# First attention of a two-layer block: the order of an iteration's steps on TensorE

## What is computed

```python
q = lat @ Wq                                   # lat: layer norm of x, (4, 512, 128)
kv = jnp.concatenate([ctx, lat], axis=1) @ Wkv # ctx: layer norm of the context, (4, 32, 128)
k, v = jnp.split(kv, 2, axis=-1)               # split_heads: 16 heads of 64
dots = jnp.einsum('bhid,bhjd->bhij', q, k) * scale
attn = jax.nn.softmax(dots, axis=-1)
out = jnp.einsum('bhij,bhjd->bhid', attn, v)   # heads joined again
return out @ Wout
...
x = x + first_attention(ctx, layernorm(x))
x = x + experts_b(layernorm(x))                # one expert of 8 for a row
x = x + second_attention(layernorm(x), ctx)
x = x + experts_d(layernorm(x))                # two experts of 8 for a row
```

## Time and profile before

| | |
|---|---|
| median of 3 runs | 792.72 us (792.16 to 794.59) |
| profiled execution, span | 798.2 us |
| PE busy | 713.8 us (89%) |
| DVE busy | 491.6 us (62%) |
| ACT busy | 366.9 us (46%) |
| POOL busy | 378.2 us (47%) |
| mean granted clock of PE | 0.948 |
| chain that ended last | PE 75%, DVE 8%, issue 6% |

### The profile page before, as it was taken

The page is one execution under the profiler, slowest core; times in us unless marked ns, Lnnn a source line. Parts: engine busy times, 40 slices in busy tenths (PEclk is TensorE's granted clock), DMA queues, the critical chain, the costliest instruction groups (busy, mean ns, idle before and its releaser), DMA issues.

```text
span 798.2 us, 13900 instructions
## 1 busy us (share of the span) xinstructions
PE 713.8 (89%) x4626; PEld 414.0 (52%) x4626; DVE 491.6 (62%) x1077; ACT 366.9 (46%) x572; POOL 378.2 (47%) x369
## 2 busy tenths in 40 slices
PE   4899999999999999999999999987995587659991
PEld 4655556545556545555545455454664244326660
DVE  4655484595594875675775666664442477746673
ACT  5465554564654553654554643432332543314440
POOL 6254453553563573464375454524222314765552
PEclk9999999999999999999999999999998688569996
...
DMA packets 69132, 50.45 MB, mean 63 GB/s; under 512 B 4068, under 2 KB 62312, under 8 KB 69064
## 3 DMA queue, kind: packets, MB, share of 16 engines
...
...
## 4 chain that ended last, share of the span: by engine, by line
PE 75%; DVE 8%; issue 6%; POOL 4%; ACT 3%; DMA 2%; another core or an unknown queue 1%; SPq 1%; DVEq 0%; POOLq 0%; ACTq 0%
PE PSUM L1602 14%; PE PSUM L1634 13%; PE PSUM L1444 7%; PE PSUM L1569 5%; PE PSUM L1469 4%; PE PSUM L1700 4%; PE PSUM L1403 4%; PE PSUM L1407 3%; PE PSUM L1409 2%; PE PSUM L1408 2%; PE PSUM L1583 2%; PE PSUM L1576 2%; PE PSUM L1620 2%; PE PSUM L1664 2%; POOL results_d L643 2%
## 5 line engine op out<-in xcount | busy, mean ns | idle before, releaser
L838 ACT ACTIVATE PT<-PSUM 128x1024 f32<-128x1024 f32 x128 | 128.7, 1025 | 134.2 <-PE PSUM L1602 133.9
L671 POOL TENSOR_TENSOR PSUMS<-PT 128x1024 f32<-128x1024 f32 x32 | 76.1, 2378 | 210.6 <-ACT PT L838 171.6
L671 POOL TENSOR_TENSOR PSUMS<-PSUMS,PT 128x1024 f32<-128x1024 f32 x62 | 149.7, 2415 | 16.6 <-ACT PT L838 9.7
L1235 DVE TENSOR_REDUCE TOPS<-PSUM 128x2 f32<-128x1024 f32 x128 | 152.0, 1220 | 7.4 <-PE PSUM L1569 7.0
L1634 PE MATMUL PSUM<-PT,BIG 128*64 128x512 f32 x512 | 130.6, 611 | 0.6 <-issue 0.6
L1444 PE MATMUL PSUM<-BIG,XGT 128*128 x170 | 86.5, 614 | 2.4 <-issue 1.6
L1225 DVE TENSOR_TENSOR KL<-PSUM,KH 128x512 fp32r<-128x512 f32 x32 | 22.1, 692 | 68.0 <-ACT KH L816 67.5
L1189 DVE TENSOR_TENSOR SIL<-SIL,PSUM 128x256 f32<-128x256 f32 (+1 forms) x62 | 32.1, 518 | 48.0 <-ACT SIL L758 45.4
L1569 PE MATMUL PSUM<-KH,QH 64*128 64x512 f32 x256 | 58.0, 449 | 3.9 <-DVE QL L1228 3.6
L1634 PEld LDWEIGHTS PSUM<-PT,BIG 128*64 128x64 f32 x512 | 28.4, 135 | 54.0 <-issue 52.5
L1602 PE MATMUL PSUM<-QH,KH 64*128 64x512 f32 x256 | 54.9, 424 | 1.0 <-DVE QL L1228 0.8
...
## 6 DMA issues: line engine op xcount, KB each, us to landing
...
```

The costliest lines, as they stand in the source:

```text
L671: pool.tensor_tensor(PSUMS[:, i % 2], PTT[:, i % 2, 0] if kt == 1 else PSUMS[:, i % 2], PTT[:, i % 2, kt], ALU.add).then_inc(s_ps, 1)
L838: act.activation(PTT[:, i % 2, kt], PSUM[:, place:place + 2, :], ACT.Exp, scale=DH ** -0.5).then_inc(s_exp, 1)
L1235: dve.tensor_reduce(TOPS[:, c, 0, :], PSUM[:, place:place + 2, :], AX.X, ALU.max).then_inc(s_max, 1)
```

## The change

`ITERATION` is written anew. In the words of its names an iteration on PE is now: V, qk, mt, P0, P2, PC, the small steps of router and norm (128x128 but for PC); then p0 p1 p2 p3; then OUT, rows, CS; then t0 s0 t1 s1 t2 s2 t3 s3 t4. `max_turn` is split: DVE's part becomes `max_joined` (mj) at the end of the iteration, and the turn itself (mt) comes behind the next iteration's qk. `one_over` is split into the copy on ACT (`one_half`), four reciprocals spread over the iterations k+1 and k+2 (k = 4(g+1)), and the low part on DVE (`one_low`), which gets a wait for the former group's `spread`. `context_sums` and `context_add` take one half in iteration k and one in k+1; `spread`, `out` and `add` move from k+1 and k+2 to k+3. Steps of norm and router move by up to an iteration. Because qk of a group's first pair now comes before CS of the group before it, the queries' copy gets a fifth place, QF1.

```diff
--- before.py
+++ after.py
@@ -105,7 +105,7 @@
 
 
         with ExitStack() as queries:
-            QF = queries.enter_context(nc.sbuf_tensor("QF", [P, GROUP, S], F32))
+            QF4 = queries.enter_context(nc.sbuf_tensor("QF4", [P, GROUP, S], F32))
             TOPROW = queries.enter_context(nc.sbuf_tensor("TOPROW", [P, GROUP, S], F32R))
         BIG = sb("BIG", 3, KT * INNER)
         V = BIG[:, 1:3, :].rearrange("p k (t n) -> p k t n", t=KT)
@@ -169,6 +169,7 @@
             QL = sb1("QL", 2, S)
             KH = sb1("KH", 2, S)
             KL = sb1("KL", 2, S)
+            QF1 = first.enter_context(nc.sbuf_tensor("QF1", [P, S], F32))
 
         W2ALL = sb("W2ALL", E * F_B)
         SIL = sb("SIL", 3, BANK)
@@ -317,8 +318,7 @@
 
 
         ITERATION = (
-            "E A B PC CA0 C CA1 O0 ADD CS V qk p0 p1 t0 s0 t1 p2 t2 D s1 t3 p3 t4 P0 P2 s2 s3 rows mt O1 OUT "
-            "O2 O3").split()
+            "O C V qk mt P0 P2 PC B E A CA R p0 p1 D p2 p3 OUT ADD rows CS t0 s0 t1 s1 H t2 s2 t3 s3 t4 mj RL").split()
 
         beside = [{} for _ in range(ALL + 1)]
 
@@ -326,56 +326,60 @@
             beside[i].setdefault(at, []).append((name, a))
         for g in range(2 * B):
 
-            put(GROUP * g + GROUP - 1, "CS", "context_scores", g)
-            for half in range(2 if g < 2 * B - 1 else 0):
-                put(GROUP * (g + 1) + 1, "PC", "context_sums", (g, half))
-                put(GROUP * (g + 1) + 1, f"CA{half}", "context_add", (g, half))
+            k = GROUP * (g + 1)
+            put(k - 1, "CS", "context_scores", g)
+            if g == 2 * B - 1:
+                break
+            for half in range(2):
+                put(k + half, "PC", "context_sums", (g, half))
+                put(k + half, "CA", "context_add", (g, half))
+            put(k, "H", "one_half", g)
+            put(k + 1, "O", "one_over", (g, 0))
+            put(k + 2, "O", "one_over", (g, 1))
+            put(k + 2, "R", "one_over", (g, 2))
+            put(k + 2, "R", "one_over", (g, 3))
+            put(k + 2, "RL", "one_low", g)
+            put(k + 3, "P0", "spread", GROUP * g)
+            put(k + 3, "P2", "spread", GROUP * g + 2)
+            put(k + 3, "OUT", "out", g)
+            put(k + 3, "ADD", "add", g)
         for b in range(B + 1):
             i = b * PAIRS
-            if 2 <= b:
-                put(i, "A", "r0_slot", b - 2)
-                put(i, "D", "r0_send", b - 2)
             if b == B:
                 break
             if b + 1 < B:
-                put(i, "E", "a_stats", b + 1)
-                put(i, "A", "a_rstd", b + 1)
-                put(i + 1, "D", "a_out", b + 1)
+                put(i + 1, "E", "a_stats", b + 1)
+                put(i + 1, "A", "a_rstd", b + 1)
+                put(i + 2, "D", "a_out", b + 1)
                 put(i + 3, "C", "a_turn", b + 1)
                 put(i + 3, "D", "a_split", b + 1)
                 for kt in range(KT):
                     put(i + 4 + kt, "V", "values", (b + 1, kt))
-            for g in (2 * b - 1, 2 * b):
-                if g >= 0:
-
-                    k = GROUP * (g + 1) + 1
-                    for c in range(4):
-                        put(k, f"O{c}", "one_over", (g, c))
-                    put(k + 1, "P0", "spread", GROUP * g)
-                    put(k + 1, "P2", "spread", GROUP * g + 2)
-                    put(k + 1, "OUT", "out", g)
-                    put(k + 2, "ADD", "add", g)
             if b > 0:
                 put(i + 4, "E", "r0_stats", b - 1)
                 put(i + 4, "A", "r0_rstd", b - 1)
-                put(i + 4, "D", "r0_out", b - 1)
-                put(i + 5, "D", "r0_turn", b - 1)
+                put(i + 5, "D", "r0_out", b - 1)
+                put(i + 6, "C", "r0_turn", b - 1)
                 put(i + 6, "B", "r0_logits", b - 1)
-                put(i + 6, "C", "r0_top", b - 1)
-                put(i + 7, "A", "r0_hot", b - 1)
-                put(i + 7, "D", "r0_run", b - 1)
+                put(i + 6, "B", "r0_top", b - 1)
+                put(i + 6, "A", "r0_hot", b - 1)
+                put(i + 7, "C", "r0_run", b - 1)
+                put(i + 7, "A", "r0_slot", b - 1)
+                put(i + 7, "D", "r0_send", b - 1)
 
         first_top = [("top", (0, c)) for c in range(TOPS_OF)]
         order = [("qk", 0), ("context_keys", 1)] + first_top[0:2] + [("values", (0, 0))] + first_top[2:4] + [("values", (0, 1))]
-        order += first_top[4:] + [("max_turn", 0), ("context_kept", 1), ("counters", 0)]
+        order += first_top[4:] + [("max_joined", 0), ("max_turn", 0), ("context_kept", 1), ("counters", 0)]
 
         instead = [[("values", (0, 2))], [], [("values", (0, 3))], [("context_values", 0), ("spread_rounded", 0)]]
         for i in range(ALL):
             for at in ITERATION:
                 if at[0] == "s":
                     order.append(("scores", (i, int(at[1]))))
-                elif at in ("qk", "mt") and i + 1 < ALL:
-                    order.append(("qk" if at == "qk" else "max_turn", i + 1))
+                elif at in ("qk", "mj") and i + 1 < ALL:
+                    order.append(("qk" if at == "qk" else "max_joined", i + 1))
+                elif at == "mt" and i:
+                    order.append(("max_turn", i))
                 elif at[0] == "t" and i + 1 < ALL:
                     order.append(("top", (i + 1, int(at[1]))))
                 elif at[0] == "p":
@@ -392,8 +396,8 @@
 
         b = B - 1
         rest = [("e_tables", 0), ("kv_copies", 0), ("context_sums", (last, 0), 2, 2), ("rows", ALL - 1), ("context_add", (last, 0)),
-                ("one_over", (last, 0))] + [("pv", (ALL - 1, kt)) for kt in range(KT)]
-        rest += [("one_over", (last, c)) for c in range(1, 4)] + [("context_sums", (last, 1), 4, 2), ("context_add", (last, 1)),
+                ("one_half", last), ("one_over", (last, 0))] + [("pv", (ALL - 1, kt)) for kt in range(KT)]
+        rest += [("one_over", (last, c)) for c in range(1, 4)] + [("one_low", last), ("context_sums", (last, 1), 4, 2), ("context_add", (last, 1)),
                  ("e_tables", 2), ("masks", 0)]
         rest += [("kv", 0), ("kv_kept", 0), ("spread", GROUP * last, 0, 2), ("spread", GROUP * last + 2, 4, 2), ("ex", 0), ("ex", 1),
                  ("ek", 0), ("ek", 1), ("e_tables", 3), ("out", last, 0, 1), ("add", last), ("eg", 0), ("r0_stats", b), ("r0_rstd", b),
@@ -421,6 +425,10 @@
 
         scored = [(name, a) for name, a, place, banks in order_a if name in ("scores", "context_scores")]
         SCORED = {step: i + 1 for i, step in enumerate(scored)}
+
+        def query(i):
+
+            return QF4[:, i % (GROUP + 1), :] if i % (GROUP + 1) < GROUP else QF1[:, :]
 
         def scores_of(i):
             return SCORED["scores", (i, KT - 1)]
@@ -814,9 +822,9 @@
                         act.wait_ge(s_sc, scores_of(a - 2))
                     act.activation(QH[:, a % 2, :], PSUM[:, place, :], ACT.Copy).then_inc(s_qkh, 1)
                     act.activation(KH[:, a % 2, :], PSUM[:, place + 1, :], ACT.Copy).then_inc(s_qkh, 1)
-                    if a >= GROUP:
-                        act.wait_ge(s_sc, context_of(a // GROUP - 1))
-                    act.activation(QF[:, a % GROUP, :], PSUM[:, place, :], ACT.Copy).then_inc(s_qkh, 1)
+                    if a > GROUP:
+                        act.wait_ge(s_sc, context_of((a - 1) // GROUP - 1))
+                    act.activation(query(a), PSUM[:, place, :], ACT.Copy).then_inc(s_qkh, 1)
                 elif name == "max_turn":
                     act.wait_ge(s_topt, a + 1)
                     if a >= GROUP:
@@ -849,8 +857,8 @@
                     if i >= OTS:
                         act.wait_ge(s_out, (i - OTS) // GROUP + 1)
                     act.activation(OT[:, i % OTS, :], PSUM[:, 6, :], ACT.Copy).then_inc(s_ot, 1)
-                elif name == "one_over" and a[1] == 0:
-                    g = a[0]
+                elif name == "one_half":
+                    g = a
                     act.wait_ge(s_rows, GROUP // 2 * (g + 1))
                     if g:
                         act.wait_ge(s_recl, g)
@@ -1237,7 +1245,7 @@
                         dve.tensor_reduce(TOPS[:, :, 1, :].rearrange("p t h -> p h t"),
                                           PSUM[:, place:place + 2, 0:TPB * M].rearrange("p h (t n) -> p h t n", t=TPB),
                                           AX.X, ALU.max).then_inc(s_max, 1)
-                elif name == "max_turn":
+                elif name == "max_joined":
                     dve.wait_ge(s_max, TOPS_OF * (a + 1))
                     if a:
                         dve.wait_ge(s_topt, a)
@@ -1253,12 +1261,15 @@
                         dve.tensor_tensor(REC[0:64, :], REC[0:64, :], PSUM[64:128, 7, :], ALU.add).then_inc(s_sums, 1)
                         dve.wait_ge(s_sums, g + 1)
                     dve.reciprocal(REC[0:64, cols], REC[0:64, cols]).then_inc(s_rec, 1)
-                    if c == 3:
```

(17 more changed lines are left out.)

## The result

| | before | after |
|---|---|---|
| median, same chip | 793.65 us (4 runs) | 833.63 us (831.68 to 835.61, 4 runs) |
| profiled execution, span | 798.2 us | 830.0 us |
| mean granted clock of PE | 0.948 | 0.944 |

The changed kernel takes 1.0496 times as long (95% interval 1.0466 to 1.0526): 40 us more, where 18.8 were forecast and the range ended at 821.

A forecast was written before the change was run, and what follows sets the result against it. PE's own stream bounds the kernel (busy 100.00 of 100 us). Terms -19.5 + 31 + 12.4 - 2.1 + 1 + 2.4 - 5.4 - 1 = +18.8 us on the 792.72 median gave 811.5 us; range 797 to 821.

The forecast's parts named there:

- crossings and block, net, 31 plain iterations: PE's loop: fewer shape changes save 19.5 us, waits in the block of maxima and scores cost 31 us.
- P2's wait less the crossings of P0 and P2: Behind mt: P2 waits for QL to free qk's place, 12.4 us in all; shape changes no longer needed save 2.1.
- PC, OUT, CS: Shape changes: CS loses one of its own, OUT and the split PC gain one each; plus 1 us, within 2.
- waits of before that go, last iteration: Today's waits of t1 and t4 go, minus 5.4 us; fewer crossings in the last iteration, minus 1.
- the third block: t0 to t4 at the iteration's end: s1, t3 and s3 wait for their places, 1.0 us an iteration.
- rival without waits (780): DVE and ACT free the places in time for s1, t3 and s3, so 31 us fall away: 780; chance 0.12.
- The maxima's turn: ... mt does not wait: mt behind qk: the maxima are joined 0.7 us behind t4, the projections take 1.5, so no wait.
- takers between qk and P2 are mt and P0 alone: PSUM places behind qk: the argument against P2 not waiting, a rival of 799 us with chance 0.06.
- at clock 1.00: Attention after the change: PE's busy share falls from 100 to about 93, its clock stays at 1.00.
- the reciprocals behind the router's steps (2.4): DVE, iterations 14, 22 and 30: reciprocals come 0 to 1.7 us late behind router steps; 2.4 us in all.
- Rows had 0.4 us of slack: rows ahead of the third block: GpSimd's adds end at 11.5, PE arrives at 11.9; cost 0.
- DVE comes late ... in more iterations, +10: Rival: about 14 iterations start the third block 0.5 to 1 us late, rows waits for GpSimd; 821, chance 0.12.

The follow-up runs named there:

- e5: Changed kernel with DVE's maxima over the scores reading 256 of 512 keys: 817.60 us, ratio 1.0286 to the kernel before.
- e6: Kernel before with DVE's maxima over the scores reading 256 of 512 keys: 795.27 us, ratio 1.0014.
- e8: Changed kernel with GpSimd's second and third add of each iteration over 64 of 512 columns: 813.84 us, ratio 1.0247 to before.
- e3: Changed kernel with P0 and P2 between p1 and p2 instead of behind the maxima's turn: 817.72 us, ratio 1.0306 to before.
- e2: Changed kernel with the router's counts moved from the iteration's head to behind qk and the maxima's turn: 828.29 us, ratio 1.0360 to before.
- e4: Changed kernel with 12 filler matmuls ahead of the maxima's turn in iterations 15 and 23: 834.63 us, ratio 1.0444 to before.
- e7: Changed kernel with p2 and p3 again between the turns of maxima and scores, rows ahead of them: 839.77 us, ratio 1.0506 to before.
- e12: Changed kernel reordered: pv in two visits, P0, P2 and whole context sums ahead of projections, router's counts behind them, rows late: 790.06 us, ratio 0.9953 to before.

## Why the prediction was right and wrong

| term | forecast | measured |
|---|---|---|
| crossings and block, net, 31 plain iterations | +11.5 | +8.7 |
| P2's wait less the crossings of P0 and P2 | +10.3 | +11.5 |
| PC, OUT, CS | +1 | +8.6 |
| router and norm: their steps, and waits ahead of max_turn and P0 | +2.4 | +13.5 |
| pv at the lower clock | 0 | +6.7 |
| waits of before that go, last iteration | -6.4 | -8.6 |
| sum | +18.8 | +40.4 |

(The terms measured come from the table by step; the plain iteration's shares, rounded, make the 0.4 too much. "Waits of before that go" is what is left of top and scores, +8.5, less 31 plain shares of 0.55.)

**Right: the direction, the block and P2.** The starts of the third block came out within 0.07 us, each of six, and its waits as 0.92 where 0.99 was derived. e5 and e6 show the mechanism: the same edit gives 2.1% in after, nothing in before. The rival without waits (780) falls; it needed a block wait below 0.4 us. The Trainium skill, page "TensorEngine Tiling (Array Packing)", section Performance Considerations, warned of the emptying of PSUM, and the trace agrees: 1.22 us of DVE and 1.02 of ACT stand behind each turn. P2's wait was derived rightly too, 1.88 a time: in e8, where P0 comes on time, P0 and P2 take 2.98 instead of 1.12 us six times over.

**Luck in one row: +10.3 forecast, +11.5 measured.** In after P2's six waits are smaller than derived, since P0 is late itself: spread is 8.4 us above before in the six iterations, of which e3 takes back 6.9. The other 3.1 are iteration 31, where the prediction had 0.5 for the router's counts and P2 waited 1.9 for PLACE, at the lower clock. The row agrees because one error made up for another.

**Wrong: "OUT and the split PC gain one each", 0.15 for a PC.** I counted the split as a second visit. It is a second full run, 1.02 us for half the matmuls, +7.7. The trace of before held 16 records in 1.04, and the code says which rows each half uses; I did not put the two together.

**Wrong: "The maxima's turn: ... mt does not wait", and P0 at nothing.** mt does not wait for the maxima, right; but it waits for its place. I had followed the place of P2 through its takers ("takers between qk and P2 are mt and P0 alone"), and not those of mt and P0 in the iterations in which the change puts the router's counts or the norm's turn at the head, each a taker more. That gave PLACE (5.6 us of idle time ahead of mt) and XT (2.8 ahead of P0). RECS (3.7) is no place: P0 reads it, and one_low makes it late. In e3 P0's waits, XT and RECS, are gone (6.5 in max_turn); in e2 those for PLACE (11 us, with the moved subtraction in it). And e8 shows that the place alone is not enough: same order, no such wait, once DVE is not late.

**Wrong: the durations of moved DVE instructions.** The sum has no term for one_low or the router's subtraction, which leaves them as long as in before. one_low stands at the iteration's end now, beside GpSimd's adds, and takes 2.67 us instead of 1.05; the router's subtraction takes 2.23 instead of 0.18. The trace of before held the hint, a median of 1052 ns beside a shortest of 685 for the same instruction: the seven long ones began 1.9 us into an add of 2.4 and ended 0.55 behind it; in after they begin 0.2 to 0.3 us into one. I had not asked what ran beside them. e8 shows the size: 20 us of the 40 hang on it, waits and clock included, so this and the two terms above overlap.

**Wrong: "at clock 1.00".** Idle stretches of 2.79 and 1.49 us close to each other brought the lower level, in iterations 15 and 23; e4 shows that it follows the idleness and is worth 4 to 5 us in those two. Over the loop the clock was 0.98, and all slow pv together cost 6.7.

**Wrong the other way:** the reciprocals behind the router's steps (2.4) are in no wait of the list. Rows had 0.4 us of slack and did not wait, right as put; in e7, where it had none, it waited 15.7.

The rival "DVE comes late ... in more iterations, +10" named the right engine and the wrong victim: not t0 but max_turn and P0. Its price came from a slack of half a us, and not from what a late DVE costs in places and clock; hence the range's end at 821 for 833.6.

What stays open: how much of e8's 20 us would be left with P0 and P2 moved as well (the two edits were not run together but in e12); how much of e2's 11 us is the place and how much the subtraction; and why the clock's fall was whole in iterations 15 and 23, partial in 11, and absent in e8 behind idle stretches of 1.64.
